# Two mixture-of-experts stages on one Trainium2 core: the experts' outputs added by matrix products instead of by scattering DMAs

## What is computed

```python
capacity = max(1, int(Sz * CAP_FACTOR / E) + 1)          # 257 of 1024 tokens, 8 experts
scores = jax.nn.softmax(jnp.einsum('bsd,ed->bse', x, router_w), axis=-1)
gate_vals, sel_idx = jax.lax.top_k(jnp.swapaxes(scores, 1, 2), capacity)
tokens = x[b_idx, sel_idx]                               # 2 batches x 8 experts x 257 rows
h = jnp.einsum('becd,edh->bech', tokens, w1) + b1[None, :, None, :]
h = jax.nn.gelu(h, approximate=False)                    # 512 hidden units
y = jnp.einsum('bech,ehd->becd', h, w2) + b2[None, :, None, :]
out = jnp.zeros_like(x).at[b_idx, sel_idx].add(y * gate_vals[..., None])
```

## Time and profile before

| | us |
|---|---|
| median of 3 runs | 1100.13 |
| lowest and highest | 1097.97 and 1104.66 |
| the profiled execution, its own time | 1106.95 |
| span of its trace (first to last instruction) | 1105.2 |
| PE busy in the span | 859.2 (78%) |
| DVE, ACT, POOL busy | 612.0, 466.6, 425.3 |

### The profile page before, as it was taken

One profiled execution on the slowest core, in us unless ns is written; L12 is line 12 of the kernel. 1 busy time (PEld: TensorE's weight loads), 2 busy tenths in 40 slices (PEclk: granted clock), 3 DMA queues, 4 the chain that ended last, 5 costly groups with the idle time before them and its releaser, 6 DMA issues. The chain is left out here.

```text
span 1105.2 us, 15650 instructions
## 1 busy us (share of the span) xinstructions
PE 859.2 (78%) x5651; PEld 564.2 (51%) x5651; DVE 612.0 (55%) x1386; ACT 466.6 (42%) x956; POOL 425.3 (38%) x654
## 2 busy tenths in 40 slices
PE   2879999999986126989748899999998911599993
PEld 1545565566545016878634344444443511489883
DVE  4776677677744742333246877777774376223240
ACT  1425666666663002343223566666665300233340
POOL 1342355553330024687624122222221100646865
PEclk9989999999998557888669899999996655565695
DMA  3752343211114201442226420000000150133322
GB/s 94 214 150 54 119 116 87 80 45 51 59 40 145 86 15 46 101 92 30 23 45 172 125 77 30 31 30 2 2 1 1 48 183 3 46 84 84 54 23 19
DMA packets 58815, 74.83 MB, mean 68 GB/s; under 512 B 13033, under 2 KB 45617, under 8 KB 58354
## 3 DMA queue, kind: packets, MB, share of 16 engines
q1 hardware_dynamic: 41234, 60.47, 18.3%
q0 software_dynamic: 12288, 8.70, 6.1%
q10 hardware_dynamic: 5216, 4.66, 1.4%
HBM read 42.40 MB, written 30.29 MB: 66 GB/s over the span
## 5 line engine op out<-in xcount | busy, mean ns | idle before, releaser
L1050 ACT ACTIVATE b_pt<-b_banks 128x512 f32<-128x512 f32 (+1 forms) x320 | 154.7, 558 | 106.3 <-PE b_banks L964 106.0
L1417 PE MATMUL f_banks<-f_w2r,f_hr 128*128 128x128 f32 (+1 forms) x960 | 141.2, 306 | 18.7 <-issue 9.4
L1073 DVE TENSOR_REDUCE a_mlate<-a_banks 128x2 f32<-128x1024 f32 (+3 forms) x120 | 125.0, 1079 | 51.5 <-PE a_banks L902 32.9
L1073 DVE TENSOR_REDUCE b_mlate<-b_banks 128x2 f32<-128x1024 f32 (+3 forms) x120 | 125.6, 1079 | 33.2 <-PE b_banks L902 17.4
L1417 PEld LDWEIGHTS f_banks<-f_w2r,f_hr 128*128 128x128 f32 (+1 forms) x960 | 128.4, 205 | 25.0 <-issue 20.5
L1468 ACT ACTIVATE f_h<-f_banks,b_t 128x258 f32<-128x258 f32 x128 | 54.2, 467 | 184.4 <-issue 128.2
L1487 DVE TENSOR_TENSOR f_hr<-f_h,f_hr 128x516 fp32r<-128x516 f32 x64 | 43.2, 688 | 152.7 <-ACT f_hr L1474 122.2
L1294 POOL DMA_INDIRECT f_xg<-scratch_table,f_index x64 | 63.0, 984 | 156.7 <-DVE f_index_left L1608 137.8
L964 PE MATMUL a_banks<-a_q,a_k 121*128 121x512 f32 (+3 forms) x384 | 117.8, 384 | 5.4 <-DMA a_q<-a_mt 4.5
L964 PE MATMUL b_banks<-b_q,b_k 64*128 64x512 f32 (+3 forms) x384 | 102.9, 432 | 9.4 <-ACT b_pt L1050 7.9
L1050 ACT ACTIVATE a_q_hl<-a_banks 128x512 f32<-128x512 f32 (+1 forms) x160 | 81.8, 557 | 66.8 <-PE a_banks L964 65.3
(11 more groups left out here) (245 smaller groups left out, 1279.3 us busy)
## 6 DMA issues: line engine op xcount, KB each, us to landing
scratch_w<-a_tab SPq DMA_DIRECT2D x16, 512.0 KB
f_w1r<-scratch_w SPq DMA_DIRECT2D x16, 512.0 KB, 4.6
f_w2r<-scratch_w SPq DMA_DIRECT2D x16, 512.0 KB, 4.3
a_rot<-in_w SPq DMA_DIRECT2D x16, 256.0 KB
a_q<-scratch_q SPq DMA_DIRECT2D x8, 384.0 KB
a_k<-scratch_k SPq DMA_DIRECT2D x8, 384.0 KB
scratch_q<-b_q_hl SPq DMA_DIRECT2D x24, 128.0 KB, 2.7
b_q<-scratch_q SPq DMA_DIRECT2D x32, 96.0 KB
```

Source lines behind the costliest of these rows:

```text
L1050: act.activation(pt[at % NPT][:, h, 0:cols], st[u % NST][:, 0:cols], ACT.Exp, scale=scale).then_inc(exp_done, 1)
L1073: last = dve.tensor_reduce(dst, src, AX.X, ALU.max, negate=True)
L1417: pe.matmul(to, of(hp, j), w2r[e % WB][:, wp, j * D:(j + 1) * D], start=(j == 0 and i == 0), stop=False)
```

## The change

**Search.** The tokens stay on the partitions, so the scores aren't turned. A step compares all scores with three trial values in two instructions of 192 elements (`compare`), and the counts over the partitions are eight accumulated products with a matrix of ones (`count`). The scans give way to products with a triangular matrix (`prefix`).

**Places.** The marks, the products and `index` are made for one batch at a time. Those of batch 1 are made inside the loop, at passes 0 to 2.

**The loop** goes batch by batch (`b, e = divmod(q, NE)`), with the matrices of all eight experts on chip for both batches. `turn_x` moves to the head of a pass, `hidden` uses two banks of PSUM, and its four groups alternate with the halves of `output` of the pass before. The left-over row has a group of 13 products in every pass.

**The sums.** Nothing is scattered. For each pass POOL makes two matrices of zeros and ones (`one_hot`: for each of the 128 rows of a tile, a one at its token, 1024 columns), ACT and DVE make the gated high and low parts of the output, and PE adds them into eight tiles of PSUM: `combine(q - 2)`, 32 products of 128 columns in every pass. The left-over rows move through SP (`y_one`, `y_left`) and are added once for each batch (`combine_left`, 16 products). DVE adds the sums to `x` (`add`). The base's stores, the scatters and the loads back are gone. The zeros and ones have two buffers, and `one_hot(q)` waits for `combine(q - 2)`.

The loops of POOL and PE, and the functions that they call; what is left out is the search, the marks, and the declarations:

```diff
@@ gpsimd
-        pool.wait_ge(table_in, 16 * (NCH + 1))
-        pool.wait_ge(index_ready, 2)
-        for e in range(GB):
-            gather(e)
-        pool.wait_ge(based, 16 * NCH)
-        for e in range(NE):
-            scatter(e)
-            if e + GB < NE:
-                gather(e + GB)
+        def gather(q):
+            b, e = divmod(q, NE)
+            if q >= GB:
+                pool.wait_ge(gated, q - GB + 1)
+            for i in range(2):
+                pool.indirect_dma_start(
+                    xg[q % GB][:, i, :], None, m.scratch["table"],
+                    bass.IndirectOffsetOnAxis(ap=index[:, b, e, i:i + 1], axis=0)).then_inc(g_in[q % GB], 16)
...
+        def one_hot(q):
+            b, e = divmod(q, NE)
+            if q >= 2:
+                pool.wait_ge(spread_used, q - 1)
+            for i in range(2):
+                last = pool.tensor_scalar(spread[q % 2][:, i, :], tokens[:, :], local[:, b, e, i:i + 1], None, ALU.is_equal)
+            last.then_inc(spread_ready, 1)
...
+        for q in range(NQ):
+            b, e = divmod(q, NE)
+            if q % NE == 0:
+                pool.wait_ge(index_ready, 4 * (b + 1))
+            gather(q)
+            if q % NE == 0:
+                gather_left(b)
+            if q:
+                one_hot(q - 1)
+            if q % NE == 1:
+                pool.tensor_scalar(spread_left[b][:, :], tokens[0:NE, :], local_left[:, b:b + 1], None, ALU.is_equal
+                                   ).then_inc(left_spread, 1)
+        one_hot(NQ - 1)
@@ tensor
+        def turn_x(q):
+            b, e = divmod(q, NE)
+            if q:
+                pe.wait_ge(x_split, q)
+            pe.wait_ge(g_in[q % GB], 32 * (q // GB + 1))
+            pe.wait_ge(left_in[b], 16)
...
+        def combine(q):
+            b, e = divmod(q, NE)
+            pe.wait_ge(spread_ready, q + 1)
+            pe.wait_ge(gated, q + 1)
+            if b and e == 0:
+                pe.wait_ge(added, NCH // B)
+            for t in range(QT):
+                for c in range(2):
+                    for part in range(2):
+                        last = pe.matmul(sum_ps[t], spread[q % 2][:, c, t * P:(t + 1) * P], ys[q % 2][part][:, c, :],
+                                         start=(e == 0 and t % TPC == 0 and c == 0 and part == 0), stop=False,
+                                         skip_group_check=True)
+            last.then_inc(spread_used, 1)
...
         turn_x(0)
         for q in range(NQ):
-            e, b = divmod(q, B)
-            for j in range(HB):
-                hidden(q, j)
-            if b == 0 and e + 1 < NE:
-                turn_x(e + 1)
+            if q + 1 < NQ:
+                turn_x(q + 1)
+            hidden(q, 0)
+            hidden(q, 1)
+            if q == NE + 2:
+                combine_left(0)
             if q:
-                output(q - 1)
-        output(NQ - 1)
+                output(q - 1, 0)
+            hidden(q, 2)
+            if q:
+                output(q - 1, 1)
+            hidden(q, 3)
+            if q >= 2:
+                combine(q - 2)
+            if q == PLACES:
+                places(1)
+            if q == PLACES + 1:
+                indices(1)
+        output(NQ - 1, 0)
+        output(NQ - 1, 1)
+        combine(NQ - 2)
+        combine(NQ - 1)
+        combine_left(1)
```

More of the change, by code:

```diff
@@ L401 @@
 IDLE = {"project": {"a": 0, "b": 36}, "attend": {"a": 34, "b": 10}, "piece": 2, "sum": 8, "turn": [(0, 0, 10, 0), (4, 4, 22, 0)],
[L402 removed]
+        "logits": [(8, 6, 3, 3), (4, 4, 3, 3)], "search": 6, "marks": 20, "places": 5, "gather": 15}
 def keep_busy(pe, m, to, count):
@@ new lines, in prefix @@
+        def prefix(to, marks):
+            pe.matmul(to, m.peers[:, 1, :], marks[:, :, :, :].rearrange("p b t e -> p (b t e)"), start=True, stop=False,
+                      skip_group_check=True)
+            for t in range(QT - 1):
+                last = pe.matmul(by_expert(to)[:, :, t + 1:, :], m.peers[:, 0, :],
+                                 marks[:, :, t:t + 1, :].to_broadcast([P, B, QT - 1 - t, NE]), start=False, stop=(t == QT - 2),
+                                 skip_group_check=True)
+            return last
@@ new lines, in search @@
+        def search():
+            for i in range(n_search):
+                keep_busy(pe, m, h_ps[0][:, 0:2 * P], IDLE["search"])
+                pe.wait_ge(marked, i + 1)
+                count(mask[:, :, :, :, :].rearrange("p b n t e -> p (b n) t e"), B * 3).then_inc(counted, 1)
+            pe.wait_ge(marked, n_search + 1)
+            count(above, B)
+            prefix(rank_ps, tied).then_inc(counted, 1)
+            pe.wait_ge(marked, n_search + 2)
+            prefix(pos_ps, take).then_inc(counted, 1)
@@ new lines, in places @@
+        def places(b):
+            pe.wait_ge(hi_ready, b + 1)
+            for t in range(QT):
+                pe.wait_ge(id_ready, QT * b + t + 1)
+                if t % (QT // 2) == 0:
+                    pe.wait_ge(lo_ready, 2 * b + 1 + t // (QT // 2))
+                last = pe.matmul(places_ps, mark_id[:, t, :], mark_lo[:, t * NE:(t + 1) * NE, :].rearrange("p e l -> p (e l)"),
+                                 start=(t == 0), stop=(t == QT - 1))
+            last.then_inc(places_ready, 1)
@@ L1421, in tensor, with combine_left @@
+        def combine_left(b):
+            pe.wait_ge(left_spread, b + 1)
+            pe.wait_ge(left_gated, b + 1)
+            for t in range(QT):
+                for part in range(2):
+                    last = pe.matmul(sum_ps[t], spread_left[b][:, t * P:(t + 1) * P], ys_left[part][:, :], start=False,
+                                     stop=(part == 1), skip_group_check=True)
+                if t % TPC == TPC - 1:
+                    last.then_inc(summed, 1)
         if projected:
@@ L1610, in vector @@
-        count_above(m.steps)
-        for i in range(len(SHIFTS)):
-            step(i)
-        ties()
-        places()
-        split_x(0)
-        for q in range(NQ):
-            e, b = divmod(q, B)
-            low(q, 0, 2)
-            low(q, 2, 4)
-            if b == 0 and e + 1 < NE:
-                split_x(e + 1)
-            if q:
-                gate(q - 1)
-        gate(NQ - 1)
+        dve.wait_ge(scored, 2)
+        scores = by_batch(score[:, :, :])
+        over_trials = lambda t: t.rearrange("p b (o e) -> p b o e", o=1).to_broadcast([P, B, 3, NE])
```

530 lines of the change are left out of this document (288 added, 242 removed).

## The result

| | before | after |
|---|---|---|
| median of four runs, us | 1102.39 | 1634.06 |
| lowest and highest | 1097.97, 1111.72 | 1631.69, 1634.72 |
| span of the profiled execution | 1105.2 | 1632.7 |
| mean granted clock of TensorE | 0.839 | 0.715 |

The changed kernel takes 1.480 times as long (95% interval 1.470 to 1.490). The forecast was 1544 us with a range up to 1625. Sign and mechanism are as forecast; the time lies 90 us above the forecast and 9 above the range.

A forecast was written before the change was run, and what follows sets the result against it. It took PE to bound the expert loops, with no engine full overall. Stage changes of +227.1 and +222.5 and -6 for search and places gave 1106.95 + 443.6 = 1550.6 us profiled, so 1544 predicted, range 1400 to 1625.

The forecast's parts named there:

- The order on POOL and the wait: Expert loops: gathers queue behind one-hots waiting for combine, so PE waits 6.2 us in 12 passes a stage, 24 in all.
- The price of a comparison: POOL's 128x1024 one-hot, priced at 1.04 us by a cast of as many elements; two of them, 2.08 us, in each wait.
- the other end: Alternative price of POOL's one-hot: 2.56 us, from a two-input product with 512 elements at 1.28 us.
- the two-input rival: One-hots cost the two-input rate, so POOL's wait grows by 3.0 us in 24 passes: 1617 us; chance 0.09.
- The level: PE's clock in both loops: low level (near 0.50) for whole passes, 18.65 us of work, 24.85 us with the wait.
- the 36 us of the earlier trace: Kernel before, from 980 us: PE busy 35.88 us yet at the low level; the forecast's ground for low passes.
- The work of a pass: PE's work per loop pass without the wait: 10.5 us high, 18.65 low, of which combine 3.95 or 7.33.
- The sum for a stage: First gather to next attention: 386.5 us against 159.4, second stage 390.5 against 168.0, after 8 us off for passes 1 and 2.
- Search and places: Before the loops: a step 2.3 us (2.2 to 2.6) against 1.88, +6 in 15 steps; in all -3 us a stage.
- That the level comes back within a pass: Rival: the wait is there but the high level returns within passes; half the passes' time high gives about 1415 us; chance 0.11.
- That POOL runs ahead: Rival: one-hots don't hold back gathers, so PE is dense from pass 1 and the level high: 1142 us; chance 0.05.
- That a combining product becomes cheap enough: Rival, not slower: combine products fall from 0.123 to 0.082 us or below, giving 1100 us; chance 0.05.

The follow-up runs named there:

- The cast kernel: Changed kernel (1634 us) with each 128x1024 comparison on POOL replaced by a plain cast of the same size; 1537.2 us, 1.393 of the kernel before.
- the kernel where it had not fallen: Comparisons moved to VectorE, left-over rows one group later, 14 of batch 0's 16 left-over products left out; 1127.4 us, 1.021 of the kernel before.
- the small steps: On wide products with comparisons on VectorE (1088.2 us): left-over rows one group later, 1078.0 us; then also more filler products at the start, 1074.5 us.
- one kernel (1189 and 1246 us): Kernel with comparisons on VectorE (1251.3 us), batch 0's left-over rows combined one group later; 1189.3 and 1246.2 us in its two runs.
- the best version: Changed kernel with wide combining products, comparisons on VectorE, left-over rows one group later and TensorE kept busy at the start; 1074.5 us, 0.980 of the kernel before.

## Why the prediction was right in kind and 90 us short

**The order on POOL and the wait: right.** Place, chain and count are as drawn. 12 passes in each stage wait, and gathers ahead of the comparisons take the waits away.

**The price of a comparison: the step that failed.** The prediction wrote "I take 1.04, since the one-hot reads one tensor and a single number per partition, and keep 2.56 as the other end." It measures 2.86, above both ends, so the two on the path took 5.67 us where the sum has 2.08. Twice 1.82 in 24 waits is 87 us, and 1544 + 87 = 1631; measured 1634. The cast kernel shows that the rest of the sum holds. The nearest row was chosen by what an instruction reads, though a cast applies no operation to its elements and a comparison does; and the other end, a doubled row of 512 elements, was taken for an upper bound that nothing made one. The Trainium skill (GPSIMD Engine Reference, Elementwise — side-by-side cycle accounting) measures GpSimd at 1.96 times VectorE's time for a two-input addition; here the comparison is at 3.8 times, 2.86 to 0.75.

**The range: too narrow at the top.** It ended at 1625, 8 us above the two-input rival. That rival named the right term and was still too cheap by 17.

**The level: right, and its reason too.** Low for the whole of the 12 passes and the end, as the 36 us of the earlier trace rows had suggested. Of passes 1 and 2, for which 8 us were deducted, pass 1 was low and the work of pass 2 high: 13.4 and 10.7 us, together what the forecast has after the deduction. That it does not come back by itself in work of this shape is now shown: 68 us of full PE at 0.50, and the same stretch at 1.00 in the kernel where it had not fallen.

**The work of a pass: right.** 18.65 us low in the changed kernel (28.57 less the wait of 9.92; forecast 18.65) and 18.4 where nothing waits, 10.15 high (10.5). `combine` is 6.7 and 3.5 us from its start to the next instruction's, 0.210 and 0.110 a product, where the output rows had promised 0.229 and 0.123.

**The sum for a stage: short by the comparisons.** From the first gather 437.2 us (397.9 to 835.1) against 386.5, and 440.3 against 390.5. Of the 50 us, 43.7 are the comparisons of the twelve waits; the other 6 to 7 are mostly comparisons in the head of the stage, where 13.0 us were forecast until pass 1 and 19.7 passed.

**Search and places: sign right, a third of the size.** A step takes 1.94 and 1.96 us in the two stages in place of 2.3, below the 2.2 that the prediction gave as the least, since the handovers are shorter than priced; the eight products are at 0.50, inside my 0.4 to 0.8. One step in the timeline of the changed kernel:

```profile
359.78 0.63 DVE L1668 TENSOR_TENSOR f_mask<-f_score,f_trial 128x192 bf16<-128x192 f32 x2
...
360.46 0.50 PE L1366 MATMUL f_banks<-f_mask,peers 128*128 128x48 bf16 x8 [0.24 <-DVE f_mask L1668]
...
361.07 0.21 DVE L1676 TENSOR_SCALAR f_enough<-f_banks 128x48 f32<-128x48 f32 x1 [0.34 <-PE f_banks L1366]
...
361.80 0.63 DVE L1668 TENSOR_TENSOR f_mask<-f_score,f_trial 128x192 bf16<-128x192 f32 x2
```

From the scores to the first gather it is 40.4 us against 49.1, so 8.7 and 8.4 saved in the two stages where I took 3. Start to start a step was 1.90 and 1.92 before, so the 15 steps cost 0.6 us more and not 6, which is nearly all of the difference.

**The rivals.** That the level comes back within a pass did not happen with these products and did with wide ones. That POOL runs ahead came out only in the kernel that reorders it, at 1284 and not 1142, since the level is lost midway. That a combining product becomes cheap enough was ruled out for the narrow shape (0.110 against the 0.082 it needed; 81 ns by the Trainium skill's TensorE: Matmul & The Clock Gate, Back-to-back issue gap, isn't reached). The way below the kernel before was another one: 8 products of 0.23 us do the work of 32 of 0.110.

**Where the 532 us came from.** Moving the comparisons off the gathers' queue takes the time to 1251: 383 us, the wait and a good part of the low level that it brings. A level that holds takes it to 1127: 124 us. The last 25 us over the kernel before are, as far as the sums go, the narrow products' work less what the change saves elsewhere. Wide products win back 53, of which the small steps are 14.

## What to carry to other kernels

Ask of each instruction that waits what is queued behind it on its engine, and whether that has to wait as well: here two gathers stood behind a comparison, and their order alone was worth 350 us. Price an elementwise operation on GpSimd by a row with the same operation, and where there is none make the range reach well past the dearest row. On TensorE, look for short waits and for products with few rows in a dense loop, since a few of them can cost more by the clock than by their own duration, and try few products with long moving operands in place of many with short ones.

## What was not expected of the hardware

- `tensor_scalar` with `is_equal`, 128x1024 in 32 bits: 2.86 us on GpSimd and 0.75 on VectorE. For 8 partitions in place of 128 it is as slow, shown by the group of the left-over rows in the best version:

```profile
L1322 POOL TENSOR_SCALAR f_spread_left<-f_tokens,f_local_left 8x1024 fp32r<-8x1024 f32 x4 | 11.4, 2850 | 0.1
```

- TensorE at 1.2 GHz for 68 us without an idle moment, and at 2.4 GHz over the same stretch when 2 us of eight-row products ahead of it were gone.
- Which way it goes can differ between the two stages of one execution, and with it two runs of one kernel (1189 and 1246 us).
- Products of 128 and of 8 rows in turn begin every 0.25 us, those of either kind alone every 0.12.

- In the loops with a narrow `combine` a wait of 1 to 3 us can also cost the level for the rest of a stage, or not: 1.04 us did, 1.12 us did not.

What stays open: why the level falls at one such place and not at the next. Within the loops with a narrow `combine` it fell only in or behind a wait of 1 us or more or at the small products. With two small products in place of sixteen it did not fall in pass 10, and at the ends of both stages, where all sixteen stood, it did. Why it came back behind some blocks of longer products and not behind others is open as well.
